# A fused attention and expert kernel: the work of its first two batches in a new order on all five engines

## What is computed

```python
x = layer_norm(ctx, ln1_w, ln1_b)                  # 128 keys from the context
lat = layer_norm(layernorm(x_in), ln2_w, ln2_b)    # 128 queries from x
lat = lat * (1.0 + scale[:, None, :]) + shift[:, None, :]
q = lat @ Wq.T
k, v = split(concat(x, lat) @ Wkv.T)               # 256 keys: context and lat
w = softmax(q k / 8)                               # 16 heads of 64
x1 = x_in + (w v) @ Wo.T
...
x = layernorm(x1)
out = x1 + silu(x @ ws1) * (x @ ws3) @ ws2 + one_routed_expert_of_8(x)
```

## Time and profile before

| what | value |
|---|---|
| median of 3 runs | 688.5 us (688.04 to 688.54) |
| profiled execution | 687.99 us, its span 686.3 us |
| PE busy | 675.2 us, 98% of the span |
| DVE, ACT, POOL busy | 69%, 63%, 40% of the span |

### The profile page before, as it was taken

The page is one execution under the profiler, slowest core; times in us unless marked ns, Lnnn a source line. Parts: engine busy times, 40 slices in busy tenths (PEclk is TensorE's granted clock), DMA queues, the critical chain, the costliest instruction groups (busy, mean ns, idle before and its releaser), DMA issues. The chain is left out here.

```text
span 686.3 us, 17910 instructions
## 1 busy us (share of the span) xinstructions
PE 675.2 (98%) x5935; PEld 629.7 (92%) x5936; DVE 470.6 (69%) x970; ACT 431.6 (63%) x1166; POOL 271.7 (40%) x428
## 2 busy tenths in 40 slices
PE   8899999999999999999999999999999999999997
PEld 8789899899998999989989988898899999999997
DVE  6787877877877788787797667366636676444443
ACT  4888888888788788888887864332434553222222
POOL 1853243252342343424557541047520454423333
PEclk9999999999999999999999999999999999999999
DMA  7645455555455445545546433003658999888870
GB/s 277 185 120 147 124 140 147 132 142 149 115 145 149 124 134 145 143 122 136 154 120 171 116 97 123 9 1 91 168 189 255 312 351 294 257 262 262 258 244 6
DMA packets 77935, 111.76 MB, mean 163 GB/s; under 512 B 28732, under 2 KB 45758, under 8 KB 77632
## 3 DMA queue, kind: packets, MB, share of 16 engines
q1 hardware_dynamic: 66016, 92.73, 45.4%
q0 software_dynamic: 8864, 18.38, 9.6%
q10 hardware_dynamic: 3008, 0.03, 0.3%
HBM read 63.74 MB, written 16.67 MB: 117 GB/s over the span
## 5 line engine op out<-in xcount | busy, mean ns | idle before, releaser
L1029 PE MATMUL PS<-BIG 128*128 128x256 f32 (+1 forms) x1164 | 199.1, 325 | 3.3 <-ACT V L630 2.4
L1029 PEld LDWEIGHTS PS<-BIG 128*128 128x128 f32 x1164 | 167.5, 192 | 20.2 <-issue 5.4
L648 ACT ACTIVATE PR<-PS,NMX 128x256 f32<-128x256 f32 x256 | 118.4, 475 | 40.9 <-DVE NMX L833 40.9
L2086 PE MATMUL PS<-XST,W 128*128 128x128 f32 x1012 | 116.7, 275 | 0.0
L491 POOL DMA_DIRECT2D PT<-PR x128 | 65.1, 514 | 126.2 <-DVE PR L845 82.1
L2086 PEld LDWEIGHTS PS<-XST,W 128*128 128x128 f32 x1012 | 115.0, 192 | 0.1
L657 ACT ACTIVATE PR<-PR,RINV 128x256 f32<-128x256 f32 x256 | 105.9, 509 | 0.0
L845 DVE STREAM_TRANSPOSE PR<-PR 128x512 f32<-128x512 f32 x124 | 82.0, 689 | 4.3 <-ACT PR L657 1.2
L833 DVE TENSOR_REDUCE NMX<-PS 128x4 f32<-128x1024 f32 x64 | 75.5, 1199 | 0.1
L1581 POOL DMA_INDIRECT out_x<-YS,WHO x23 | 31.7, 1376 | 85.0 <-DVE YS L1948 75.6
L1047 PE MATMUL PS<-KVF,WQ 128*128 128x128 f32 x512 | 63.8, 278 | 0.0
(11 more groups left out here) (187 smaller groups left out, 1105.2 us busy)
## 6 DMA issues: line engine op xcount, KB each, us to landing
PT<-PR SPq DMA_DIRECT2D x368, 64.0 KB, 2.3
W<-in_w SPq DMA_DIRECT2D x29, 640.0 KB
W<-in_w SPq DMA_DIRECT2D x21, 768.0 KB
PT<-PR POOLq DMA_DIRECT2D x128, 64.0 KB, 2.5
turned<-CXN SPq DMA_DIRECT2D x15, 256.0 KB, 2.0
INT<-turned POOLq DMA_DIRECT2D x56, 64.0 KB, 2.7
xs_sorted<-C SPq DMA_DIRECT2D x26, 128.5 KB, 3.1
W<-in_w SPq DMA_DIRECT2D x8, 352.0 KB
```

The lines of the kernel that those rows point to most:

```text
L648: last = act.activation(probs, logits, ACT.Exp, bias=NMX[:, g, own, p % 2:p % 2 + 1], accum_out=SUM[:, p, own:own + 1])
L1029: last = pe.matmul(dst, stat(s, k), mov(m, k), start=n == 0, stop=n == len(todo) - 1)
L2086: last = pe.matmul(h[:, P * c:P * (c + 1)], lhs13(W13[par], k, c), XST[par][:, :, k, :], start=k == 0, stop=k == KD - 1)
```

## The change

Only the order of the lists is changed, and nothing is added or removed.

- PE: in batch 0 `q_unit(2)` goes ahead of `k_unit(2)`; in batch 1 `k_unit(4)` goes ahead of `times_v(0)` and `times_v(1)`, so that `q_unit(4)` comes right behind them.
- ACT: in batch 0 `kv_hi(1)` and `v_all(0)` follow the first `normalise` and not the second and the last, and `q_hi(2)` goes ahead of `k_hi(2, 0, 0)`; in batch 1 `o_hi(0)` and `o_hi(1)` go behind the last `exps`.
- DVE: in batch 0 the maxima of half 1 go ahead of three of the four transposes of half 0 and `q_lo(2)` ahead of `k_lo(2)`; in batch 1 `o_lo(0)` and `o_lo(1)` go behind `norm_rows(3)`; in all batches but 0 `q_lo(h+1)` comes after the second maximum.
- POOL: `kv_lo(1)` goes ahead of the first two of the eight splits of the output weights (`wo_split`, L514 and L516).

```diff
--- before.py
+++ after.py
@@ -552,10 +552,8 @@
                     values_lo(k, i)
 
             pool.wait_ge(v_kvf, 2)
-            for k in range(2):
-                wo_split(k)
             kv_lo(1, 1)
-            for k in range(2, 4):
+            for k in range(4):
                 wo_split(k)
             keep_probs(0, 0)
             norms(2)
@@ -682,26 +680,32 @@
                     exps(h, b, 0, p)
                 for p in range(HP):
                     normalise(h, 0, p)
-                    if not last and p == (1 if first else HP - 1):
+                    if not last and p == (0 if first else HP - 1):
                         kv_hi(b + 1, 1 - par)
-                for tile in range(2):
-                    v_all(h, 0, par, tile)
-
-            def half_1(b, par, first=False, final=False):
+                    if p == (0 if first else HP - 1):
+                        for tile in range(2):
+                            v_all(h, 0, par, tile)
+
+            def half_1(b, par, first=False, second=False, final=False):
                 h = 2 * b + 1
                 exps(h, b, 1, 0, final)
-                if not first:
+                if not first and not second:
                     o_hi(h - 3, b - 1, 0)
                 exps(h, b, 1, 1, final)
-                if not first:
+                if not first and not second:
                     o_hi(h - 2, b - 1, 1)
+                if first:
+                    q_hi(h + 1, 0)
                 if not final:
                     k_hi(h + 1, 0, 0)
                 exps(h, b, 1, 2, final)
                 if not final:
                     k_hi(h + 1, 0, 1)
                 exps(h, b, 1, 3, final)
-                if not final:
+                if second:
+                    for H in range(2):
+                        o_hi(h - 3 + H, b - 1, H)
+                if not first and not final:
                     q_hi(h + 1, 0)
                 for p in range(HP):
                     normalise(h, 1, p, final)
@@ -709,9 +713,9 @@
                     for tile in range(2):
                         v_all(h, 1, par, tile)
 
-            def batch(b, par, first=False, last=False):
+            def batch(b, par, first=False, second=False, last=False):
                 half_0(b, par, first, last)
-                half_1(b, par, first, last)
+                half_1(b, par, first, second, last)
 
             def keys_hi(H):
                 act.wait_ge(d_wk[H], 16)
@@ -740,7 +744,7 @@
                 values_hi(k)
 
             batch(0, 0, first=True)
-            batch(1, 1)
+            batch(1, 1, second=True)
             batch(2, 0)
             with act.Fori(0, LOOPS - 1) as i:
                 batch(2 * i + 3, 1)
@@ -904,8 +908,11 @@
             def half_0(b, par, first=False, second=False, last=False):
                 h = 2 * b
                 row_max(h, 0)
-                q_lo(h + 1, 1)
+                if first:
+                    q_lo(h + 1, 1)
                 row_max(h, 1)
+                if not first:
+                    q_lo(h + 1, 1)
                 k_lo(h + 1, 1, 0)
                 k_lo(h + 1, 1, 1)
                 inverse_sums(h, 0)
@@ -917,19 +924,25 @@
                 transpose_blocks(h, 0, 0)
                 if not first and not last:
                     modulate(b + 1, 1 - par)
+                if first:
+                    for g in range(2):
+                        row_max(h + 1, g)
                 for p in (1, 2, 3):
                     transpose_blocks(h, 0, p)
 
             def half_1(b, par, first=False, second=False, final=False, norm=True):
                 h = 2 * b + 1
-                for g in range(2):
-                    row_max(h, g)
                 if not first:
+                    for g in range(2):
+                        row_max(h, g)
+                if not first and not second:
                     o_lo(h - 3, 0)
                 if norm:
                     norm_stats(b + 2)
-                if not first:
+                if not first and not second:
                     o_lo(h - 2, 1)
+                if first:
+                    q_lo(h + 1, 0)
                 if not first and not second:
                     expert_input(b - 2)
                 if not final:
@@ -944,8 +957,12 @@
                 if norm:
                     norm_rows(b + 2)
                 inverse_sums(h, 1)
+                if second:
+                    for H in range(2):
+                        o_lo(h - 3 + H, H)
                 if not final:
-                    q_lo(h + 1, 0)
+                    if not first:
+                        q_lo(h + 1, 0)
                     for p in (0, 1):
                         transpose_blocks(h, 1, p)
                 else:
@@ -1149,16 +1166,23 @@
                 for tile in range(2):
                     v_unit(h, 0, par, tile)
 
-            def half_1(b, par, first=False, final=False):
+            def half_1(b, par, first=False, second=False, final=False):
                 h = 2 * b + 1
                 logits(h, 1)
+                if first:
+                    q_unit(h + 1, b + 1, 0, 1 - par)
+                if second:
+                    for i in range(2):
+                        k_unit(h + 1, b + 1, 0, 1 - par, i)
                 if not first:
                     times_v(h - 3, b - 1, 0, 1 - par)
                     times_v(h - 2, b - 1, 1, 1 - par)
                 if not final:
-                    for i in range(2):
-                        k_unit(h + 1, b + 1, 0, 1 - par, i)
-                    q_unit(h + 1, b + 1, 0, 1 - par)
+                    if not second:
+                        for i in range(2):
+                            k_unit(h + 1, b + 1, 0, 1 - par, i)
+                    if not first:
+                        q_unit(h + 1, b + 1, 0, 1 - par)
                     if early(h, 2):
                         pe.wait_ge(p_wv_lo, KD * (h + 1))
                 for tile in range(2):
```

## The result

The changed kernel takes 697.3 us in the median of 4 runs (696.92 to 697.79), the kernel before 688.5 us (688.04 to 689.24). The ratio is 1.0131, 95% interval 1.0115 to 1.0146: slower by 1.3%, 1.3 us more than the forecast of 696.0 and inside its range. The profiled execution took 697.79 us against 687.99, which is 9.8 us; the medians differ by 8.8 us. What follows is read from the two profiled executions.

What follows compares the result with a forecast made beforehand. PE was taken to bound the kernel, busy in 675 of 686 us. 687.99 us + 5.0 (`q_unit(4)` starting later) + 3.0 (half clock behind two stops) = 696.0 us; range 691.9 to 698.1.

Steps and rivals of the forecast that it cites:

- Stop ahead of `k_unit(2)` filled, clock kept: Batch 0, PE: `q_unit(2)` fills the 2.42 us stop ahead of `k_unit(2)`, and the clock stays at 1.00.
- New stop ahead of `v_unit(1)`: Batch 0, PE: without `q_unit(2)` as cover, PE waits some 1.9 us for `k_lo(2)`; no clock cost counted.
- Batch 1 paced by ACT and DVE: Batch 1: PE does not set the pace; `exps(2, 0)` starts at 38.9, `kv_hi(2)` ends at 47.9, `kv_lo(2)` at 49.2.
- stop 2: Batch 1, PE ahead of `q_unit(4)`: 4.4 us for `o_lo`, behind `norm_rows(3)`, POOL's `norms(3)` and `keep_probs(1, 0)`.
- Stop ahead of `v_unit(2)`: Batch 1, PE: a stop of 0.8 us until `k_lo(3)` is done near 41.6, as before.
- Stop 1: Batch 1, PE ahead of `k_unit(4)`: 2.9 us for POOL's `kv_lo(2)`, which `times_v` used to cover.
- the dip: A fall of PE's granted clock to 0.50 behind a stop, counted as 1.5 us each.
- The clock: Batch 1, PE: half clock follows the stops of 2.9 and 4.4 us, 1.5 us each, 3.0 in all.
- the sum: Whole kernel: 687.99 + 5.0 for the later `q_unit(4)` + 3.0 for half clock = 696.0 us.

Runs made afterwards that it cites:

- e1_batch0: The changed kernel with batch 1's second half back in its old order on PE, ACT and DVE: 686.73 us, ratio 0.9977 to the kernel before.
- e6_before_fill: The kernel before with 9 unread identity matmuls ahead of `k_unit(2)` on PE: 688.74 us, ratio 1.0007.
- e9_norms2_first: `e1_batch0` with `norms(2)` moved ahead of `keep_probs(0, 0)` on POOL: 686.71 us, ratio 0.9977 to the kernel before.
- e8_pe_old: The changed kernel with batch 1's old order on PE alone, both `times_v` ahead of `k_unit(4)`: 692.81 us, ratio 1.0058 to the kernel before.
- e3_olo_first: The changed kernel with batch 1's `o_lo(0)` and `o_lo(1)` ahead of `norm_rows(3)` on DVE: 692.16 us, ratio 1.0057 to the kernel before.
- e4_norms_first: The changed kernel with `norms(3)` ahead of `keep_probs(1, 0)` on POOL in batch 1: 692.80 us, ratio 1.0069 to the kernel before.
- e5_fill_both: The changed kernel with unread identity matmuls on PE, 11 ahead of `k_unit(4)` and 17 ahead of `q_unit(4)`: 693.42 us, ratio 1.0072 to the kernel before.
- e2_batch1: The kernel before with only batch 1's second half in the new order on PE, ACT and DVE: 698.61 us, ratio 1.0151.

## Why the prediction was right, step by step

- **Stop ahead of `k_unit(2)` filled, clock kept**: right. `q_unit(2)` at 25.12 and `k_unit(2)` at 26.93, no idle time, clock 1.00 from 25 to 30.
- **New stop ahead of `v_unit(1)`**, 1.9 us expected, 1.36 measured: right in place and cause, 0.5 us too long. It did not take the clock down here; in the profile of `e1_batch0` one of 1.83 did.
- **Batch 1 paced by ACT and DVE**: right, and shown by `e6_before_fill`. `kv_hi(2)` was worked out to end at 47.9 and ended at 48.2; `kv_lo(2)` at 49.2 and 49.55. The 0.3 us come from the gain at its start, which I sized at 1.1 us: the first maximum came at 38.09 instead of 38.77, 0.7 us earlier, and `exps(2, 0)` at 39.30 and not 38.9. DVE's `norm_rows(2)`, before and after, shows why:

```profile
33.45 0.87 DVE L777 TENSOR_SCALAR CXN<-RC,MV,RS 128x256 f32<-128x256 f32 x1
33.57 0.47 DVE L781 TENSOR_SCALAR CXN<-RC,MV,RS 128x256 f32<-128x256 f32 x1 [1.07 <-POOL RS L468]
```

It starts no earlier, since it now stands 1.07 us for POOL's `norms(2)`, which comes behind `keep_probs(0, 0)`: a chain over POOL like that of stop 2, one batch earlier, for which the prediction took off only 0.5 us. `e9_norms2_first` moves `norms(2)` ahead, and there the first maximum comes earlier.
- **Stop ahead of `v_unit(2)`**, 0.8 us expected, 1.34 measured: mis-sized, mostly because `exps(2, 0)` and with it `k_lo(3)` came 0.4 to 0.5 us later than worked out. It cost nothing here, since `k_unit(4)` then waits for `kv_lo(2)` anyway.
- **Stop 1**, 2.9 us expected, 2.79 measured, on the `kv_lo` named. `e8_pe_old` takes it away: `q_unit(4)` then starts 5.2 us earlier (57.12 against 62.30, from the same start of `logits(3)`), 1.55 of it the dip, 2.8 the stop, and the rest because the second stop is 3.5 us, set by ACT, and not 4.4. The median falls by 4.6.
- **Stop 2**, 4.4 us expected and measured, on the chain named; `e3_olo_first` and `e4_norms_first` cut it at two different engines with the same effect.
- **The clock** is the mis-sized term. I counted 1.5 us for each dip, from the one example in the trace. The first cost 1.55 (4.53 - 2.98). The second cost 2.6, since half clock lasted from 60.8 to 67.6, twice as long as the 3.4 us of the earlier trace rows. Together that is 4.15 us and not 3.0, 1.15 of the 1.8 us by which the sum missed the profiled execution (697.79 against 696.0). Why the second lasted twice as long is not shown. By the Trainium skill, "TensorE: Matmul & The Clock Gate", in its list of terms, the penalty is the throttled time times one minus the share of pulses passed: 6.8 us of half clock give 3.4. The trace shows 2.6, because 1.5 us of it lay where PE stood anyway.
- **The rest** of the miss: `q_unit(4)` was 62.30 - 1.55 = 60.75 without the first dip, against 60.2 worked out, 0.55 us late, most of it from the start of batch 1. The median was missed by 1.3 us and not 1.8, since the profiled execution is the slowest of the changed kernel's four runs.

## What to carry to other kernels

A unit of work that is moved to fill a stop leaves the place where it was cover; look up what that place waited for before moving it. When an instruction is moved down an in-order queue, list what the instructions now ahead of it wait for, across engines: the last input of `o_lo` was ready when ACT's `o_hi` ended, near 58.6, and the pair ran from 60.9, because `norms(3)` stood behind transfers that POOL had still to issue. And count a stop on TensorE with the half clock that may follow it: where nothing later absorbed it, it cost 1.5 to 2.9 us behind stops of 1.8 to 4.4 us here, and 11 and 17 cheap matmuls in the stops took it away (`e5_fill_both`).

## What was unexpected of the hardware

- Half clock came in two lengths: 3.4 us behind stops of 1.8 to 2.8 us, and 6.8 us behind the stops of 3.5 and 4.4 us of `e8_pe_old`, the changed kernel and its repetition; behind the 4.40 us of the profiled execution of `e2_batch1` it was 3.4 again. It cost about 1.5, 2.6 to 2.9 and 1.7 us there. It can begin while PE still stands: at 60.8 us of the changed kernel's span, with PE idle until 62.30.
- Whether a stop of 1.4 to 1.8 us is followed by it differs from execution to execution: one of 1.83 us was in `e1_batch0` and one of 1.83 us was not in `e2_batch1`; 1.68 us was not (`e4_norms_first`).
- The first units start at different times from execution to execution: `logits(1)` at 23.44 us of the span in the kernel before and at 24.28 in `e6_before_fill`, with the same lists ahead of it. Some of the spread of single runs, 2 us and more, may lie there, and some in the dips; how much in each was not tested.
- A `norm_rows` instruction of DVE (128x256) took 0.40 or 0.41 us in batch 1's second half, where POOL did no arithmetic, and 0.87 or 0.89 us where it ran beside a `tensor_tensor` of POOL's `wo_split` (DVE from 33.45 and POOL from 33.44 us before, 33.96 and 33.97 after). It is so in both kernels and explains no difference between them.
